# Last attention block of a fused layer: denominators and division moved ahead of the preceding block's router products and row norms

## What is computed

```python
x = x + attn(layernorm(x), w_qkv, w_out, decay)     # 16 heads of 32
x = x + moe(layernorm(x), gate_w, w_gate, w_up, w_down, sw_gate, sw_up, sw_down)

# attn: q, k, v = split(x @ w_qkv); q, k = elu(q) + 1, elu(k) + 1
# s_kv[t] = decay * s_kv[t-1] + k[t] * v[t];  s_k[t] = decay * s_k[t-1] + k[t]
# den = max(sum_over_head(q * s_k), 1e-6)
# out = (q * s_kv / den) @ w_out
# moe: 8 experts of 352, the best 2 by softmax(x @ gate_w), weighted,
#      + shared = silu(x @ sw_gate) * (x @ sw_up) @ sw_down   (704 wide, in two halves of 352)
```

## Time and profile before

| | us |
|---|---|
| median of 3 runs | 739.93 (736.96 to 740.67) |
| the profiled execution's own time | 738.84 |
| its span, first to last instruction | 736.8 |
| PE busy in it | 655.2 (89%) |
| DVE busy in it | 441.9 (60%) |
| mean granted TensorE clock | 0.977 of full |

### The profile page before, as it was taken

One profiled execution on the slowest core, in us unless ns is written; L12 is line 12 of the kernel. 1 busy time (PEld: TensorE's weight loads), 2 busy tenths in 40 slices (PEclk: granted clock), 3 DMA queues, 4 the chain that ended last, 5 costly groups with the idle time before them and its releaser, 6 DMA issues.

```text
span 736.8 us, 11499 instructions
## 1 busy us (share of the span) xinstructions
PE 655.2 (89%) x3677; PEld 422.1 (57%) x3678; DVE 441.9 (60%) x808; ACT 235.7 (32%) x353; POOL 215.4 (29%) x234
## 2 busy tenths in 40 slices
PE   3979889879899599899998999999899899989982
PEld 2757567558577365465655656655455555545551
DVE  6879888987997661786876976433322232232221
ACT  4343421242342212446665664411111111111110
POOL 6100111101102026333432333143344433334431
PEclk9999999999999799899999999999999999999998
DMA  6840003512433577975855316367666666676662
GB/s 215 280 127 16 15 19 83 161 39 58 117 84 86 132 170 205 273 179 149 183 150 147 58 29 79 66 114 129 128 118 121 120 120 123 125 128 118 118 96 39
DMA packets 111235, 86.87 MB, mean 118 GB/s; under 512 B 79280, under 2 KB 86448, under 8 KB 111200
## 3 DMA queue, kind: packets, MB, share of 16 engines
q1 hardware_dynamic: 88848, 43.94, 25.0%
q0 software_dynamic: 12272, 27.34, 20.8%
q10 hardware_dynamic: 10080, 15.14, 6.8%
HBM read 44.45 MB, written 23.33 MB: 92 GB/s over the span
## 4 chain that ended last, share of the span: by engine, by line
DMA 33%; PE 31%; DVE 16%; issue 12%; ACT 2%; POOL 2%; SPq 2%; POOLq 1%; DVEq 0%; ACTq 0%
DMA out_dram<-y_job,job_tok 26%; PE ring L378 12%; PE ps_y L504 5%; PE ps_g L504 5%; PE ps_u L504 5%; DMA shared<-in_L_attn_w_out_dram 2%; DVE run_kv L1205 1%; DMA routed<-in_L_ffn_w_down_dram 1%; DVE routed L1347 1%; DVE run_kv L1197 1%; SPq L771 1%; PE turn_h L524 1%; DVE run_k L1193 1%; DVE xn L1167 1%; DMA x_in<-in_L_attn_x_dram 1%
## 5 line engine op out<-in xcount | busy, mean ns | idle before, releaser
L1287 DVE TENSOR_TENSOR hidT<-turn_h,hidT 128x384 f16<-128x384 f32 x71 | 39.5, 556 | 129.4 <-ACT hidT L1036 129.2
L911 POOL DMA_INDIRECT out_dram<-y_job,job_tok x39 | 61.4, 1574 | 142.1 <-DVE y_job L1638 74.8
L504 PE MATMUL ps_g<-routed,x_in 128*128 x468 | 76.5, 313 | 17.1 <-DMA x_in<-x_job 17.0
L378 PE MATMUL ring<-xnT_h,wq_h 128*128 128x512 f32 x192 | 81.1, 422 | 11.3 <-DVE run_kv L1197 4.2
L1032 ACT ACTIVATE silu<-ps_g,job_silu 128x352 f32<-128x352 f32 x39 | 21.6, 553 | 209.1 <-PE ps_g L504 209.1
L504 PE MATMUL ps_y<-routed,hidT 128*128 x351 | 82.1, 379 | 1.3 <-DVE hidT L1287 1.3
L378 PE MATMUL ring<-xnT_l,wq_h 128*128 128x512 f32 x192 | 78.1, 407 | 0.0
L378 PE MATMUL ring<-xnT_h,wq_l 128*128 128x512 f32 x192 | 77.9, 406 | 0.0
L836 POOL TENSOR_SCALAR var_eps<-mean_var 128x1 f32<-128x1 f32 x32 | 11.7, 367 | 226.4 <-DVE mean_var L1268 125.7
L504 PE MATMUL ps_u<-routed,x_in 128*128 x468 | 76.2, 313 | 0.0
L504 PE MATMUL ps_y<-shared,hidT 128*128 128x512 f16 x288 | 69.3, 387 | 7.5 <-DVE hidT L1287 7.4
(11 more groups left out here) (222 smaller groups left out, 1062.9 us busy)
## 6 DMA issues: line engine op xcount, KB each, us to landing
routed<-in_L_ffn_w_gate_dram ACTq DMA_DIRECT2D x7, 704.0 KB, 4.8
routed<-in_L_ffn_w_up_dram ACTq DMA_DIRECT2D x7, 704.0 KB, 9.0
x_res<-in_L_attn_x_dram SPq DMA_DIRECT2D x18, 256.0 KB, 3.2
out_dram<-x SPq DMA_DIRECT2D x16, 256.0 KB, 3.3
xn_scratch<-xn_hl SPq DMA_DIRECT2D x16, 256.0 KB, 2.5
out_dram<-y_job POOLq DMA_DIRECT2D x16, 256.0 KB, 4.2
x_in<-in_L_attn_x_dram SPq DMA_DIRECT2D x14, 256.0 KB, 2.7
routed<-in_L_ffn_w_down_dram ACTq DMA_DIRECT2D x7, 512.0 KB, 10.8
```

Of the source, the lines that this page charges most:

```text
L378: ins = pe.matmul(ps, a, b, start=(i == 0), stop=(i == len(steps) - 1))
L504: ins = pe.matmul(ps, a[i][:, k, :], w(j, k), start=(start and q == 0), stop=(stop and q == len(steps) - 1))
L911: pool.indirect_dma_start(out[:, :], bass.IndirectOffsetOnAxis(job_tok[:, r:r + 1], 0), y_job[:, b, :], None, compute_op=ALU.add).then_inc ...
L1287: dve.tensor_tensor(hidT[:, 1], turn_h[:, 0:FC, :], hidT[:, 0], ALU.subtract).then_inc(s["hidT_s"], 1)
```

## The change

SP's and POOL's programs are untouched. PE: `expand(3)` goes ahead of `gate(9)`, and gate(9), gate(10), gate(11) come after output(3, 0), output(3, 2) and output(3, 3). `output(3, 0)` waits for the low halves chunk by chunk. The second bank of the last block is `ps_den` instead of ring bank 1. ScalarE: `gate_silu(0)` comes first, `hi_a(3)` ahead of `hi_2(10)`. VectorE: `residual` is split into `sum_2` and `stats_2`; norm_2(9) and the statistics of tile 10 come after the reciprocal, `divide` and `lo_a` are interleaved by chunks, and lo_2(9), tile 11's sum and all later tile steps come after them.

```diff
 # PE
-last_banks = [(turn..., None), (ring[1], 1), (ring[2], 2), (ring[4], 4)]
+last_banks = [(turn..., None), (ps_den, None), (ring[2], 2), (ring[4], 4)]
 def last_bank(c, freed_by, value):
     ps, m = last_banks[c]
     if freed_by == "a_s":
-        if m is None:
+        if c == 0:
             turn_free()
+        elif c == 1:
+            pe.wait_ge(s["den_max"], NB)
         else:
             pe.wait_ge(*release[ring_use(m)])
 def output(n, j):
-    pe.wait_ge(s["al_s"], (n + 1) * KC)
+    if n < NB - 1 or j:
+        pe.wait_ge(s["al_s"], (n + 1) * KC)
...
-    split_product(ps[:, :], [((at_h[:, k, tok], at_l[:, n % 2, k, tok]), (wo_h[:, k, :], wo_l[:, k, :]))
-                             for k in chunks]).then_inc(s["out_mm"], 1)
+    for k in chunks:
+        if n == NB - 1 and j == 0:
+            pe.wait_ge(s["al_s"], n * KC + k + 1)
+        for i, (a, w) in enumerate(((at_h[:, k, tok], wo_h[:, k, :]), (at_h[:, k, tok], wo_l[:, k, :]),
+                                    (at_l[:, n % 2, k, tok], wo_h[:, k, :]))):
+            ins = pe.matmul(ps[:, :], a, w, start=(k == 0 and i == 0), stop=(k == KC - 1 and i == 2))
+    ins.then_inc(s["out_mm"], 1)
 gate(before_last)
-gate(before_last + 1)
 expand(NB - 1)
 gate_product(1, 0, 0, gate_w)
 up_product(1, 0, up_w)
+output(NB - 1, 0)
+gate(before_last + 1)
+output(NB - 1, 1)
+output(NB - 1, 2)
 gate(before_last + 2)
-output(NB - 1, 0)
-output(NB - 1, 1)
-gate(before_last + 3)
-output(NB - 1, 2)
 pe.wait_ge(s["x2_s"], last + 1)
 turn_hidden(0, True)
 output(NB - 1, 3)
-pe.wait_ge(s["x2_s"], last + 2)
+gate(before_last + 3)
+pe.wait_ge(*release[ring_use(1)])
 down_product(0, 0, shared_down(0), True, False, True)
 # ScalarE
+gate_silu(0, shared_by, True)
 hi_2(before_last + 1)
-gate_silu(0, shared_by, True)
-hi_2(before_last + 2)
 for c in chunks:
     hi_a(NB - 1, c)
+gate_silu(1, shared_by)
+hi_2(before_last + 2)
 hi_2(before_last + 3)
-gate_silu(1, shared_by)
+upper_hidT(0)
 hi_2(last)
-upper_hidT(0)
 # VectorE; residual(t) is now sum_2(t), stats_2(t); divide and lo_a take a list of chunks
-    tile_before(norm_2, 1)
-    tile_before(residual, 2)
+    if n < NB - 1:
+        tile_before(norm_2, 1)
+        tile_before(residual, 2)
 t = (NB - 2) * TPB
+sum_2(t + 2)
 denominators(NB - 1)
+norm_2(t + 1)
+hidden(0, shared_by, True)
+divide(NB - 1, (0, 1))
+lo_a(NB - 1, (0,))
+divide(NB - 1, (2,))
+lo_a(NB - 1, (1,))
+divide(NB - 1, (3,))
+lo_a(NB - 1, (2, 3))
 lo_2(t + 1)
-hidden(0, shared_by, True)
+stats_2(t + 2)
+sum_2(t + 3)
 norm_2(t + 2)
-residual(t + 3)
-divide(NB - 1)
+stats_2(t + 3)
 lo_2(t + 2)
+residual(t + 4)
 norm_2(t + 3)
-lo_a(NB - 1)
+residual(t + 5)
 lo_2(t + 3)
-residual(t + 4)
 norm_2(t + 4)
-residual(t + 5)
+residual(t + 6)
 lo_2(t + 4)
+hidden(1, shared_by)
 norm_2(t + 5)
-hidden(1, shared_by)
-residual(t + 6)
 rest_hidT(0)
```

More of the change, by code:

```diff
@@ L441, in sum_heads @@
                               start=True, stop=True, tile_position=(0, DH * cc)).then_inc(s["den_mm"], 1)
-            last_banks = [(turn[:, :, :].rearrange("p k q -> p (k q)"), None), (ring[1], 1), (ring[2], 2), (ring[4], 4)]
+            last_banks = [(turn[:, :, :].rearrange("p k q -> p (k q)"), None), (ps_den, None), (ring[2], 2), (ring[4], 4)]
             def last_bank(c, freed_by, value):
@@ L1235, in last_bank, with divide @@
             def last_bank(c):
-                return (turn[:, :, :].rearrange("p k q -> p (k q)"), ring[1][:, :], ring[2][:, :], ring[4][:, :])[c]
-            def divide(n):
-                for c in chunks:
+                return (turn[:, :, :].rearrange("p k q -> p (k q)"), ps_den[:, :], ring[2][:, :], ring[4][:, :])[c]
+            def divide(n, which=chunks):
+                for c in which:
                     i = n * KC + c
@@ L1244, in divide, with lo_a @@
                     dve.tensor_tensor(a, a, last_bank(c) if n == NB - 1 else ring[items[(n, c, "ex")] % RING][:, :], ALU.mult).then_inc(s["a_s"], 1)
-            def lo_a(n):
-                for c in chunks:
+            def lo_a(n, which=chunks):
+                for c in which:
                     i = n * KC + c
@@ L1254, in residual, with sum_2 @@
             def residual(t):
+                sum_2(t)
+                stats_2(t)
+            def sum_2(t):
                 b = t % 2
@@ L1264, in residual, with stats_2 @@
                     .then_inc(s["x2_s"], 1)
+            def stats_2(t):
+                b = t % 2
                 dve.wait_ge(s["x2_s"], t + 1)
```

## The result

The changed kernel takes **744.59 us** (median of 18 runs, 740.74 to 747.10) against 739.91 for the kernel before on the same chips: ratio **1.0073 [1.0051, 1.0094]**, slower, with the interval's lower end just above the 0.5% that can be told. The class given the most chance, within 0.5%, was wrong.

A forecast was written before the change was run, and what follows sets the result against it. Bound by PE's chain to its last gate product, with SP's queue and the two x2 buffers as second resource. +1.5 + 1.7 - 0.7 + 0.2 = +2.7 us on 739.93 gave 742.6 us; range 739.1 to 744.8, stretched to 736.5 and 745.8.

The forecast's parts named there:

- Earlier reciprocals, division by chunks: Around attention block 3: reciprocal done 1.29 us earlier, chunk waits taken as nought, PE 9 us ahead after output(3, 0).
- What is late next: Late low half 9 delays SP's transposes and stores; sums 12 to 14 wait, and PE's 9 us lead is gone.
- The cycle of 6.76 us: From a tile's low half, through SP's transpose and store, to the sum three tiles on: 6.76 us, binding twice.
- +1.5 for the down product's start: PE's down_product(0) starts at 269.4 instead of 267.83, after idling from 262.9: +1.5 us.
- +1.7 for the half clock: PE's 6.5 us idle before down_product(0) ends at half clock, costing +1.7 us; ends 0 and 2.4.
- -0.7 + 0.2 for the idle before down_product(1): PE's 0.73 us idle there is swallowed, -0.7; sum 15 brings rest_hidT(1) about 0.2 us behind PE.
- Sum at the last gate: PE's last gate product shifts by the four terms +1.5 + 1.7 - 0.7 + 0.2 = +2.7 us.
- Rival 3: Stores of x2 slow each other, each landing in 4.0 us: +4.2, 744.1 us; chance 0.20.
- the carry "unchanged" to the end: The shift of PE's last gate, +2.7 us, passes through POOL's load to the kernel's end with no slack absorbing it.
- Landings: Stores of x2 land in 3.5 us, between 2.6 and 4.0; two bind: 1.8 less, or 1.0 and 0.5 more.
- Rival 1: Short landings: stores of x2 land in 2.6 us, +0.9, 740.8 us; chance 0.25.
- Rival 2: PE's head start stays: down_product(0) follows gate(11) at 262.9, 5.6 us off, 734.3 us; chance 0.15.

The follow-up runs named there:

- Stores first: Changed kernel with SP's queue issuing the stores of x2 (with their residual loads) ahead of the transposes: 733.59 us, 0.9934 to the kernel before.
- repeats: Both kernels again, unchanged, each twice; third traces timed at 0.9989 (kernel before) and 1.0064 (changed kernel) to the kernel before.
- the second measurement: The changed kernel, unchanged, timed again against the kernel before: ratio 1.0064 [1.0040, 1.0088].
- the filled kernel: Changed kernel with 24 spare matmuls on PE in the wait before the first down product: 744.82 us, 1.0067 to the kernel before.
- low half 11 early: Changed kernel with VectorE's low half of tile 11 ahead of tile 13's sum: 740.89 us, 1.0030 to the kernel before.
- sums apart: Changed kernel with the sums of tiles 12 and 13 in buffers of their own: 742.45 us, 1.0055 to the kernel before.

## Why the prediction was right and where it was wrong

Times from the start of the head sums, predicted (from 235.01) and measured (from 236.31):

| step | predicted | measured |
|---|---|---|
| spread | 5.3 | 5.26 |
| output(3, 0) | 10.1 | 9.81 |
| low half 9 | 11.8 | 11.58 |
| gate(9) | 15.6 | 15.40 |
| sum 12 | 18.6 | 18.50 |
| sum 13 | 22.4 | 22.51 |
| low half 11 | 23.9 | 24.06 |
| sum 14 | 30.7 | 30.60 |
| down_product(0) | 34.4 | 34.37 |
| POOL's load | 49.3 | 49.64 |

- **Earlier reciprocals, division by chunks**: right, each step within 0.3 us. No chunk wait shows on PE: output(3, 0) runs without idle.
- **What is late next**: right, and shown by an experiment, not only timed. Stores first took the waits and the loss away. The cycle of 6.76 us measured 6.92, 7.14, 6.54 and 6.79 over tiles 9 to 12; the two that bind, 7.14 and 6.54, sum to 13.68 where I had 13.52.
- **+1.5 for the down product's start**: +1.55 in this pair. Against the mean of three traces each, +34.08 and +31.91, it is +2.2. **This term was too small by 0.7**: "Before it started at 267.83" took the one trace as the kernel's habit, with a second dip of the clock that its two repeats don't have.
- **+1.7 for the half clock**: 1.45 in this trace, 1.67 and 1.75 in the repeats. Right, with some luck: it was read off the clock behind the idle of 5.35 us, and there the repeats differ widely (gate product of unit 1 at 2.51, 3.70 and 2.60 us).
- **-0.7 + 0.2 for the idle before down_product(1)**: **this step failed, in its path**, and was short by 0.5. I took the 0.73 for slack that a late PE swallows, and sum 15 for what comes next. The 0.73 stands in all three traces of both kernels, and sum 15 was where I had it (+38.94, predicted +38.95). ACT's timeline of the changed kernel, then DVE's low half 14, show what it hangs on:

```profile
276.26 0.56 ACT L1040 ACTIVATE silu<-ps_g,silu_scale 128x352 f32<-128x352 f32 x1 [5.53 <-PE ps_g L512]
276.71 0.61 ACT L994 CAST xn_hl<-xn 128x512 f16<-128x512 f32 x1
```

```profile
277.35 0.69 DVE L1297 TENSOR_TENSOR xn_hl<-xn,xn_hl 128x512 f16<-128x512 f32 x1 [0.46 <-ACT xn_hl L994]
```

  ScalarE's gate_silu(2) waits for PE's own gate product, high half 14 stands behind it, and DVE's low half 14 ahead of rest_hidT(1). From high half 14 to the second down product it is 2.54 us in this trace (276.71 to 279.25) and 2.54 in that of before (272.41 to 274.95). So the idle follows PE along and swallows nothing.
- **Sum at the last gate**: +2.7 predicted, +3.0 in the pair of traces. On the means, 49.52 - 45.74 = **+3.8**: +2.2 for the start and +1.6 for the half clock, with nothing swallowed. Ratio times 739.9 gives 5.4 us (3.8 to 7.0), the second measurement 4.7 (3.0 to 6.5). So the traces' means reach the lower end. The 1 to 1.6 us left are within the intervals and stay open. They may lie behind POOL's load: from there to the end the three traces of after take 1.8 us more on the mean (457.6 against 455.8), but within each kernel these times differ by 2.4, so the traces neither confirm nor refute the carry "unchanged" to the end.
- **Landings**: the three stores that bind landed in 3.6, 3.9 and 3.3 us, near the 3.5 that I took. The changed kernel's DMA issues from 254.7 to 255.0 us show the longest:

```profile
x_res<-in_L_attn_x_dram SPq DMA_DIRECT2D x1, 256.0 KB, 3.7
out_dram<-x SPq DMA_DIRECT2D x1, 256.0 KB, 3.9
```

The Trainium skill's "DMA: Bandwidth & Descriptors", section "Anatomy of one DMA", has a fit for DMAs issued by GpSimd that gives an estimate of 2.6 us for each; these, issued by SP, took 0.7 to 1.3 more. My reading of the earlier trace rows, 2.6 us "where no other transfer was started beside it", was wrong: behind the store at 275.73 the next transpose followed at 276.26, sooner than behind the slow one at 253.20 (254.50). What the slow one had and the fast one lacked is a load of residual rows just ahead of it (252.76). Rival 3 was built on the first reading; that the load is the cause, no run shows.
- **Rival 1** (short landings) and **rival 3** (4.0 us each, +4.2): neither mechanism is what happened. Rival 3's time, 744.1, is nearest to the median, but for another reason: the base was 0.9 us too long (46.64 against a mean of 45.74), and 0.5 was swallowed on paper only. That the measured time still lies inside the forecast's range, by 0.2 us, is owed to the width of the bounds on landings and clock, neither of which was what went wrong. **Rival 2** (the head start stays, 5.6 us off) fell for this kernel. Its price was near: with sum 13 not held by a store and sum 14 by 0.85 us, stores first gave 739.09 - 733.59 = 5.5 us by the medians, 4.9 (3.0 to 6.7) by the ratio.
- **The class**: "within 0.5%" had the most chance because the forecast lay 2.7 us up, 1 us under the bound. On the mean of three traces of before it would have been 2.7 + 0.9 = +3.6, at the bound, and "slower" as likely as "same".

## What to carry to other kernels

A step that is moved to a later place takes with it what stands behind it in the queues of other engines: before moving a DVE step, read which SP entry waits for it and who needs the entries behind. Here the same change costs 0.7% of time with the old order of SP's queue and saves 0.7% with the stores put ahead of the transposes, while that order alone is worth nothing that can be told. And take the base of a small difference from several traces: one dip of the clock, present in one trace of the kernel before and absent in two, was 1.4 us, over a third of the 3.8 us by which the stretch grew.

## What I had not expected of the hardware

- Idle of the same length is not followed by the same clock. In the kernel before, the 2.04 us ahead of gate(10) were followed by half clock some 1.7 us later, 1.95 were not, nor were 0.68. In the changed kernel the same followed the 2.51 us ahead of gate(9) (the matmuls of output(3, 1) are spaced 0.43 us from 253.57 on, for 0.23). With stores first the same 2.51 us before the same gate left them at 0.23 throughout, from 250.33 to 255.46. So did the 2.52 us in the filled kernel, whose programs are those of the changed kernel up to there.
- Less idle did not mean less at half clock: 6.17 us of it was followed by 3.55 for the down product, 5.01 and 5.47 (low half 11 early, sums apart) by 4.00. In the filled kernel 24 spare matmuls took 7.35 us, not the 24 x 0.235 = 5.6 of full spacing: the clock was low in the fill itself, as its stretches of 2 us show.

```profile
264.00:266.00 2.00, 1.94 (x12) 1.65 (x13) 0.00 (x0) 0.00 (x0) 0.00 (x0) 0.55 0.88 259
266.00:268.00 2.00, 2.00 (x7) 1.53 (x7) 1.11 (x2) 0.00 (x0) 0.00 (x0) 0.60 0.04 15
268.00:270.00 2.00, 2.00 (x10) 1.64 (x9) 1.97 (x6) 0.00 (x0) 1.33 (x2) 1.00 0.00 0
```
